# First mixture of experts: unweighed bf16 one-hots, slot weights at the silu product, expert outputs added back as three bf16 parts

## What is computed

```python
E, K, H, F = (64, 6, 256, 96)
T = 2 * 128
CAP = 2 * (T * K // E)          # 48
buf = jnp.zeros((E, CAP + 1, H), x.dtype).at[se, slot].set(x[tok])[:, :CAP]
h = jax.nn.silu(jnp.einsum('ech,ehf->ecf', buf, w_gate)) * jnp.einsum('ech,ehf->ecf', buf, w_up)
out = jnp.einsum('ecf,efh->ech', h, w_down)
gathered = out[se, jnp.minimum(pos, CAP - 1)] * valid.astype(x.dtype)[:, None]
w = topk_w.reshape(-1)[order].astype(x.dtype)[:, None]
return jax.ops.segment_sum(gathered * w, tok, num_segments=Tn)
```

## Time and profile before

| what | value |
|---|---|
| median of three runs | 692.86 us |
| profiled execution | 691.79 us |
| its span, first to last instruction | 689.9 us |
| PE busy over the span | 599.5 us (87%) |
| DVE, ACT, POOL busy | 482.6, 383.2, 330.0 us |
| mean granted TensorE clock | 0.921 |
| stage of the first experts, loop of 16 groups | 188.0 to 289.9 us |

### The profile page before, as it was taken

The page is one execution under the profiler, slowest core; times in us unless marked ns, Lnnn a source line. Parts: engine busy times, 40 slices in busy tenths (PEclk is TensorE's granted clock), DMA queues, the critical chain, the costliest instruction groups (busy, mean ns, idle before and its releaser), DMA issues. The chain is left out here.

```text
span 689.9 us, 12529 instructions
## 1 busy us (share of the span) xinstructions
PE 599.5 (87%) x4685; PEld 407.8 (59%) x4685; DVE 482.6 (70%) x793; ACT 383.2 (56%) x722; POOL 330.0 (48%) x264
## 2 busy tenths in 40 slices
PE   4976899997899999988876698888988877989997
PEld 3542445444677777676752455565555565668886
DVE  4357999995565664367686899999999956433322
ACT  4227975551432222155876799999999954321110
POOL 1009999995122332033432898989899840000000
PEclk9999999997999999999995678898878889999999
DMA  8526500000936555025563888988798738900000
GB/s 345 238 74 263 228 0 1 0 1 4 298 114 209 196 175 182 11 67 152 158 183 91 166 166 155 168 137 189 135 174 156 144 63 340 385 1 1 0 1 16
DMA packets 97090, 92.89 MB, mean 135 GB/s; under 512 B 70595, under 2 KB 88323, under 8 KB 93638
## 3 DMA queue, kind: packets, MB, share of 16 engines
q1 hardware_dynamic: 84352, 85.74, 45.7%
q10 hardware_dynamic: 12678, 6.36, 3.2%
HBM read 68.59 MB, written 6.62 MB: 109 GB/s over the span
## 5 line engine op out<-in xcount | busy, mean ns | idle before, releaser
L2074 DVE TENSOR_REDUCE d_nmax<-d_psum 128x1 f32<-128x1024 f32 x128 | 152.2, 1215 | 5.8 <-PE d_psum L2230 5.8
L2230 PE MATMUL d_psum<-kst,qT 96*128 96x512 bf16 x256 | 96.6, 477 | 31.8 <-ACT d_e L2171 12.9
L528 POOL TENSOR_TENSOR b_h<-b_h,b_cb 128x1024 f32<-128x1024 f32 x32 | 88.0, 2749 | 6.5 <-DVE b_h L578 6.0
L2054 POOL TENSOR_SCALAR d_rounded<-d_e,d_lift 128x1024 f16<-128x1024 f32 x64 | 73.2, 1144 | 13.4 <-issue 7.4
L2171 ACT ACTIVATE d_e<-d_psum,d_nmax 128x1024 f32<-128x1024 f32 x64 | 71.3, 1117 | 12.7 <-DVE d_nmax L2074 12.1
L2054 POOL TENSOR_SCALAR d_rounded<-spare,d_lift 128x1024 f16<-128x1024 f32 x62 | 70.1, 1131 | 14.4 <-ACT d_lift L2175 10.2
L578 DVE TENSOR_TENSOR_SCAN b_h<-b_dA,b_psum 128x1024 f32<-128x1024 f32 x32 | 73.2, 2286 | 2.5 <-ACT b_dA L633 2.0
L2171 ACT ACTIVATE spare<-d_psum,d_nmax 128x1024 f32<-128x1024 f32 x64 | 71.3, 1118 | 1.9 <-DVE d_nmax L2074 1.9
L633 ACT ACTIVATE b_dA<-b_dtT,b_A 128x248 f32<-128x248 f32 x128 | 53.7, 490 | 33.1 <-DVE b_h L578 28.1
L2257 PEld LDWEIGHTS d_psum<-d_ident_f,d_rounded 128*128 128x128 f16 x512 | 45.4, 123 | 32.1 <-issue 21.6
L689 PE MATMUL b_psum<-b_bdiag,b_dtx 128*128 128x512 f32 x128 | 60.2, 594 | 0.8 <-DVE b_h L578 0.8
(11 more groups left out here) (430 smaller groups left out, 1168.7 us busy)
## 6 DMA issues: line engine op xcount, KB each, us to landing
c_w<-in_w0gu SPq DMA_DIRECT2D x16, 768.0 KB, 4.8
kst<-kT_scratch SPq DMA_DIRECT2D x84, 128.0 KB, 2.7
w<-in_w SPq DMA_DIRECT2D x5, 1920.0 KB, 21.3
b_cb<-c_scratch SPq DMA_DIRECT2D x4, 2048.0 KB, 7.0
c_w<-in_w0dn SPq DMA_DIRECT2D x16, 384.0 KB, 5.5
kT_scratch<-k_kT ACTq DMA_DIRECT2D x15, 384.0 KB, 2.8
a_ctx<-in_ctx SPq DMA_DIRECT2D x2, 2048.0 KB, 19.8
k_ctxT<-in_ctxT SPq DMA_DIRECT2D x12, 256.0 KB, 3.1
```

Source lines behind the costliest of these rows:

```text
L528: nc.gpsimd.tensor_tensor(hv, hv, cv, ALU.mult).then_inc(hc_ready, 1)
L2054: nc.gpsimd.tensor_scalar(tile_of(r, j), e[j], lift[t][:, f:f + 1], HALF_ULP_ONE, ALU.mult, ALU.add).then_inc(r_ready, 1)
L2074: nc.vector.tensor_reduce(nm[:, t, m:m + 1, f:f + 1], quarter(m, j).unsqueeze(1), AX.X, ALU.max, negate=True).then_inc(nm_ready, 1)
L2230: last = nc.tensor.matmul(quarter(m, j)[:, b * 512:(b + 1) * 512], qT[0:QROWS, m:m + 1, t * P:(t + 1) * P], kst[m % 2][0:QROWS, at:at + 51 ...
```

## The change

The one-hot `pick` is now padded to 64 slots per expert itself, and goes back as it is, in bf16 and unweighed, so that POOL's weighing (`pickw`) is gone. `turn_back` is moved ahead of `gate_up` and takes group `it` in place of `it-2`; it transposes in bf16. The weights are split into three bf16 parts (five new DVE instructions before the loop), and four small matmuls per group, of 6 columns each, bring each slot's weight parts to the slot's partition. DVE sums the parts (two small reductions, `wslot`) and multiplies by them in the product with the silu, which becomes two instructions. The expert outputs are split into three bf16 parts: ACT copies the first, DVE subtracts, ACT copies the second, POOL subtracts the third. `add_back` is 12 bf16 matmuls in place of 4 fp32 ones. `back` has five buffers for three.

```diff
-        pick = [sb(f"c_pick{s}", [P, TC, GRP, CAP0], BF16) for s in range(3)]
-        pickw = [sb(f"c_pick_weighed{s}", [P, TC, GRP, HALF]) for s in range(2)]
+        pick = [sb(f"c_pick{s}", [P, TC, GRP, HALF], BF16) for s in range(3)]
...
+def split_weights(nc, dve, w, parts, rests, part_ready, rest_ready):
+
+    for q in range(K_PARTS):
+        src = ([w] + rests)[q]
+        if q:
+            dve.wait_ge(rest_ready, q)
+        nc.vector.tensor_copy(parts[q], src).then_inc(part_ready, 1)
+        if q < K_PARTS - 1:
+            dve.wait_ge(part_ready, q + 1)
+            nc.vector.tensor_tensor(rests[q], src, parts[q], ALU.subtract).then_inc(rest_ready, 1)
...
+                def split_out2(grp):
+                    s = grp % 2
+                    pool.wait_ge(out1_ready, grp + 1)
+                    nc.gpsimd.tensor_tensor(out[s][:, 2], out_rest[s][:, :, :], out[s][:, 1], ALU.subtract).then_inc(out2_ready, 1)
...
                 def choose(grp):
                     if grp >= 3:
-                        dve.wait_ge(gather_done, grp - 2)
-                        dve.wait_ge(pickw_ready, grp - 2)
+                        dve.wait_ge(back_done, grp - 2)
...
-                    nc.vector.tensor_tensor(a[grp % 2][:, :, :], silu[grp % 2][:, :, :], gu_psum[:, :, F0:],
-                                            ALU.mult).then_inc(a_ready, 1)
+                    dve.wait_ge(wslot_ready, 2 * grp + 2)
+                    for q in range(PAIRS):
+                        nc.vector.scalar_tensor_tensor(a[grp % 2][:, q, :], silu[grp % 2][:, q, :], wslot[grp % 4][:, q:q + 1],
+                                                       gu_psum[:, q, F0:], ALU.mult, ALU.mult).then_inc(a_ready, 1)
...
-                    nc.vector.tensor_copy(back[grp % 3][:, :, :], st_psum).then_inc(back_ready, 1)
-
-                def keep_out(grp):
-                    dve.wait_ge(down_done, grp + 1)
+                    nc.vector.tensor_copy(back[grp % BACKS][:, :, :], st_psum).then_inc(back_ready, 1)
+                    for h in range(2):
+                        rows_ = slice(h * HALF, (h + 1) * HALF)
+                        nc.vector.tensor_reduce(wslot[grp % 4][rows_, :], ws_psum[rows_, :, h, :], AX.X,
+                                                ALU.add).then_inc(wslot_ready, 1)
+
+                def split_out(grp):
+                    s = grp % 2
+                    dve.wait_ge(out0_ready, grp + 1)
                     if grp >= 2:
-                        dve.wait_ge(added, grp - 1)
-                    nc.vector.tensor_copy(out[grp % 2][:, :, :], out_psum).then_inc(out_ready, 1)
+                        dve.wait_ge(out2_ready, grp - 1)
+                    nc.vector.tensor_tensor(out_rest[s][:, :, :], out_psum, out[s][:, 0], ALU.subtract).then_inc(out_rest_ready, 1)
...
+                def split_out0(grp):
+                    act.wait_ge(down_done, grp + 1)
+                    if grp >= 2:
+                        act.wait_ge(added, grp - 1)
+                    nc.scalar.activation(out[grp % 2][:, 0], out_psum, ACT.Copy).then_inc(out0_ready, 1)
+
+                def split_out1(grp):
+                    act.wait_ge(out_rest_ready, grp + 1)
+                    nc.scalar.activation(out[grp % 2][:, 1], out_rest[grp % 2][:, :, :], ACT.Copy).then_inc(out1_ready, 1)
...
                     for q in range(PAIRS):
                         for t in range(TC):
-                            last = nc.tensor.matmul(acc[t], back[grp % 3][:, q, t * P:(t + 1) * P], out[grp % 2][:, q, :],
-                                                    start=False, stop=(grp == NGRP - 1 and q == PAIRS - 1),
-                                                    skip_group_check=True)
+                            for n in range(K_PARTS):
+                                last = nc.tensor.matmul(acc[t], back[grp % BACKS][:, q, t * P:(t + 1) * P], out[grp % 2][:, n, q, :],
+                                                        start=False, skip_group_check=True,
+                                                        stop=(grp == NGRP - 1 and q == PAIRS - 1 and n == K_PARTS - 1))
```

More of the change, by code:

```diff
@@ L829, in moe0_stage @@
         aT = [sb(f"c_aT{s}", [F0, PAIRS, P]) for s in range(2)]
-        back = [sb(f"c_back{s}", [P, PAIRS, T]) for s in range(3)]
-        out = [sb(f"c_out{s}", [P, PAIRS, D]) for s in range(2)]
+        back = [sb(f"c_back{s}", [P, PAIRS, T], BF16) for s in range(BACKS)]
+        out = [sb(f"c_out_parts{s}", [P, K_PARTS, PAIRS, D], BF16) for s in range(2)]
+        out_rest = [sb(f"c_out_rest{s}", [P, PAIRS, D]) for s in range(2)]
+        wparts = sb("c_w_parts", [P, TC, E0, K_PARTS], BF16)
+        wrest = [sb(f"c_w_rest{q}", [P, TC, E0]) for q in range(K_PARTS - 1)]
+        wslot = [sb(f"c_w_slot{s}", [P, PAIRS]) for s in range(4)]
         shared_silu = sb("c_shared_silu", [P, TC, F0])
@@ L931, in _ @@
                 nc.gpsimd.tensor_copy(slot[:, :], slot_i[:, :]).then_inc(slots_ready, 1)
+                for s in range(3):
+                    nc.gpsimd.memset(pick[s][:, :, :, CAP0:], 0.0).then_inc(pads_ready, 1)
                 for s in range(2):
-                    nc.gpsimd.memset(pickw[s][:, :, :, CAP0:], 0.0).then_inc(pads_ready, 1)
                     nc.gpsimd.memset(xT[s][:, :, SLOTS:], 0.0).then_inc(pads_ready, 1)
@@ L1033, in _ @@
                 weigh0(nc, step, r, w_ready)
+                dve.wait_ge(w_ready, 1)
+                split_weights(nc, dve, r.w[:, :, :], [wparts[:, :, :, q] for q in range(K_PARTS)],
+                              [rest_[:, :, :] for rest_ in wrest], wpart_ready, wrest_ready)
                 for it in range(NGRP + 4):
@@ L1036, in _ @@
                         choose(it + 2)
+                    if it < NGRP:
+                        keep_back(it)
                     if 1 <= it <= NGRP:
                         multiply(it - 1)
-                    if 2 <= it <= NGRP + 1:
-                        keep_back(it - 2)
                     if 3 <= it <= NGRP + 2:
-                        keep_out(it - 3)
+                        split_out(it - 3)
                     m, at = divmod(it - QUANTIZE_AT, 2)
@@ L1182, in gather @@
                             for q in range(3):
-                                last = nc.tensor.matmul(xt_psum[:, k, :], xp[q][:, t, k * P:(k + 1) * P],
-                                                        pick[grp % 3][:, t, :, :].rearrange("p e s -> p (e s)"),
+                                last = nc.tensor.matmul(xt_psum[:, k, :].rearrange("p (e s) -> p e s", s=CAP0),
+                                                        xp[q][:, t, k * P:(k + 1) * P], pick[grp % 3][:, t, :, 0:CAP0],
                                                         start=(t == 0 and q == 0), stop=(t == TC - 1 and q == 2))
@@ L1213, in turn_back, with pair @@
                 def turn_back(grp):
-                    pe.wait_ge(pickw_ready, grp + 1)
-                    if grp >= 1:
-                        pe.wait_ge(back_ready, grp)
+                    if grp == 0:
+                        pe.wait_ge(wpart_ready, K_PARTS)
+                    else:
+                        pe.wait_ge(wslot_ready, 2 * grp)
+                    def pair(q, t):
+                        return pick[grp % 3][:, t, 2 * q:2 * q + 2, :].rearrange("p e s -> p (e s)")
                     for q in range(PAIRS):
                         for t in range(TC):
-                            last = nc.tensor.transpose(st_psum[:, q, t * P:(t + 1) * P],
-                                                       pickw[grp % 2][:, t, 2 * q:2 * q + 2, :].rearrange("p e s -> p (e s)"),
-                                                       ident[:, :])
+                            nc.tensor.transpose(st_psum[:, q, t * P:(t + 1) * P], pair(q, t), g["identb"][:, :])
+                    for q in range(PAIRS):
+                        own = slice(grp * GRP + 2 * q, grp * GRP + 2 * q + 2)
+                        for t in range(TC):
+                            last = nc.tensor.matmul(ws_psum[:, q].rearrange("p h n -> p (h n)"), pair(q, t),
+                                                    wparts[:, t, own, :].rearrange("p h n -> p (h n)"), start=(t == 0),
+                                                    stop=(t == TC - 1), skip_group_check=True)
                     last.then_inc(back_done, 1)
@@ L1251, in _ @@
                         project_second(9)
+                    if it < NGRP:
+                        turn_back(it)
                     if 1 <= it <= NGRP:
@@ L1257, in _ @@
                         turn(it - 2)
-                        turn_back(it - 2)
                     if 3 <= it <= NGRP + 2:
```

49 lines of the change are left out of this document (28 added, 21 removed).

## The result

| | before | after |
|---|---|---|
| median, runs made together | 693.79 us (4 runs, 692.32 to 695.34) | 684.4 us (4 runs, 682.1 to 686.62) |
| ratio, 95% interval | | 0.9868 [0.9827, 0.9909] |
| profiled execution, its span | 691.79, 689.9 us | 682.87, 681.1 us |
| from the first `gather` to DVE's addition to `x` | 188.0 to 289.9: 101.9 us | 184.7 to 279.8: 95.1 us |
| mean granted TensorE clock | 0.921 | 0.92 |

The forecast was 687.0 us, and the time is inside its range. A run more than 1.5% above the fastest of its kernel counts as slow and is left out of the ratios, which happens once, for three of the ten runs with the third part on DVE, the profiled one among them.

The account below looks back on a forecast made before the run. PE was taken to set the loop's pace. Savings of 6.2 us (`add_back`) and 1.0 (`turn_back`), less 0.6 (start) and 0.7 (end), gave 5.9: from 692.86 to 687.0 us, range 683.5 to 692.0.

Parts of the forecast that it names:

- `add_back`, 12 x 0.52: Bringing outputs back in iterations 4 to 15: 12 bf16 matmuls take 1.31 us instead of 1.83, 6.2 us saved.
- `turn_back`, 16 x 0.06: One-hot transposes in all 16 groups: bf16 saves more than the four new small matmuls cost, 1.0 us saved.
- The start, 0.6 lost: Loop start: PE stalls 0.5 us for the weights' third part, then 0 to 0.5 more; bounds 0.3 and 1.3.
- The end, 0.7 lost: Last iterations: 2.8 us of stalls on the output chain, less 2.1 saved by four `add_back`; bounds 0.3 and 1.5.
- A: PE in the loop: saved more, with cheaper small matmuls, `add_back` and ends; 7.6 us saved, 685.3 us; chance 0.13.
- B: Mid-loop: output chain takes over, using up 0.78 us to spare; 690.0 us if late by 0.3; chance 0.18.
- C: Next stage's start: clock falls to 1.2 GHz for 3.5 us of work, losing 1.7 us; 688.7 us; chance 0.14.
- D: Loop iterations: DVE becomes the bound through collisions with POOL, needing up to 7.0 us; 697 us; chance 0.12 with E.
- E: `add_back` on PE: three parts no cheaper than fp32, result 695 us; no share of its own, 0.12 with D.

## Why the prediction was right

The mechanism is right and some terms are off in size. The time is right, partly by luck, as the last paragraph here shows. The loop gave 6.8 us where 5.9 were forecast. Read by starts, it divides in three: from the first `gather` to that of group 3 it went from 9.90 to 10.79 us, from there to the `gather` of group 15 from 72.21 to 65.04, and from there to DVE's addition from 19.81 to 19.32.

- *`add_back`, 12 x 0.52.* Right: 1.83 to 1.32 us, 0.51. The price of 0.109 us for a matmul of 256 columns, worked out from matmuls of 128 and 192, was 0.108 in the run with two parts. The weights' reload does not show.
- *`turn_back`, 16 x 0.06.* Too small, it is 0.14, and it was one price that was wrong. The old step was worth the 0.44 that I had given it: from `turn` to `down` there were 0.79 us and now are 0.35. The new step was put at 0.38 and costs 0.30: from `gather` to `gate_up` 1.09 us became 1.39. The four transposes take 0.22, as forecast, so the small matmuls take 0.02 to 0.03 each, and not 0.04. Where a full-width `gather` follows them, at the loop's start, four take 188.53 - 188.43 = 0.10 us; in the middle 0.18, and the other 0.08 is the gap that used to stand behind `gather`. The gaps cancel, as argued. The term was worth 2.2 us, not 1.0: the largest miss.
- *The start, 0.6 lost.* The weight parts took 1.56 us, as worked out. The trace says that PE waited 0.23 us for them, but that wait is counted from the modelled end of the matmul ahead: from its start to the next there are 188.20 - 187.70 = 0.50 us, where the same step took 191.19 - 191.08 = 0.11 before, so 0.39 were lost of the 0.5 forecast. For the second `turn_back` PE did not wait. Up to the `gather` of group 3 the stretch grew by 0.89; three new steps for one old are 3 x 0.30 - 0.44 = 0.46 of it, so 0.43 was lost, which is that one stall, and within the bounds.
- *The end, 0.7 lost.* The stalls came as forecast, 0.76, 0.16 and 1.77 us against 0.7, 0.4 and 1.7. But the stretch from the `gather` of group 15 became only 0.49 us shorter. One `add_back` (0.51) and three old `turn_back` less a new one (3 x 0.44 - 0.30 = 1.02) save 1.53, so the end itself lost 1.04: the stalls of 2.69 less 4 x 0.51, and 0.39 more. The waits leave out 0.30 of this, since they too are counted from modelled ends. From start to start the stalls are 272.39 - 270.55 - 1.01 = 0.83, 275.04 - 273.79 - 1.01 = 0.24 and 278.28 - 275.04 - 1.32 = 1.92 us, 2.99 in all against 2.8 forecast. The last 0.1 lies between the start of the last `add_back` and DVE's addition: 1.51 us where its pace is 1.32, and before, for the last two, 3.75 where it is 3.66.

With these sizes, 12 x 0.51 + 16 x 0.14 - 0.43 - 1.04 = 6.9 us, against 6.8.

The rivals. **A** (7.6 saved) was right that the small matmuls are cheaper than 0.04 and wrong on the two ends; the loop's 6.8 lie in the middle between it and the forecast. **B**, the output chain: 0.78 us to spare were forecast, after 0.12 for POOL's signal to reach PE; 0.77 less 0.14 are in the timeline, and the longer chain of the experiment shows 0.66. The chain ran 0.07 us longer than laid out and the iteration was 0.06 shorter. **C**, the clock: it did not fall behind the loop in any of the four profiles of the changed kernel; it did in the run with two parts, where 3.4 us of the next stage ran at the lower level, close to the 3.5 that the prediction guessed. **D**, DVE as the bound: its collisions are there and much larger than I thought. In an iteration with both, the key product went from 0.97 to 1.66 us and one `choose` from 0.35 to 1.20, 1.54 us more, where the prediction held that collisions add about 0.3. The Trainium skill ("SBUF — State Buffer", Who interferes with whom) says that such instructions shut each other out for a whole instruction, and the trace agrees nearly: POOL's L987 began 0.04 us ahead and ended at 233.98, and the key product, 0.68 us where it runs alone, ended 0.54 after that. So DVE needed 5.40 us in these iterations and not 4.7, and had 0.13 to spare. All of PE's buffers were ready in time, so nothing came of it, but that is luck more than foresight: what helped were the lighter iterations in between, at 3.82. The experiment with the third part on DVE shows how near it was: it had to stand in DVE's queue behind the keys, and PE then waited. **E** fell with `add_back` at 1.32 us.

The whole program. All 27 runs of the changed kernel have a mean of 686.8 us, and 61 of the kernel before 691.9: 5.1 us less, a ratio of 0.993, where the loop alone would give 0.990. Outside the loop the four profiles of the changed kernel took 585.9, 591.2, 591.7 and 590.7 us, the two of the kernel before 588.0 and 589.1. Part of the first measured 9.4 us is therefore chance. In the first profile of before, the clock fell to 0.50 ahead of the stage, and in the first one after it did not:

```profile
164.00:168.00 4.00, 2.23 (x9) 1.68 (x10) 1.12 (x2) 0.00 (x0) 0.47 (x1) 1.00 0.00 0
```

The first `gather` came at 188.0 us in the one and 184.7 in the other, and between 184.8 and 188.0 in the other profiles, whose kernels are nearly alike up to there. Taken by itself, the spread of the rest, 6 us, is too large for so few profiles to say whether part of the loop's 6.8 us is given back. The timed runs say more: from their scatter, the 5.1 us are known to about 1.1 (95%), so some 1.7 us seem to be given back. The first four runs alone gained 9.4, the later ones 3 to 5, so the batches differ by more than their scatter and the bound is too narrow. But the experiments lean the same way. The loop was 14.0 us shorter with two parts and the whole 9.5 (6.1 to 12.9); with POOL's work doubled the loop was 2.3 longer and the whole 5.0 (2.8 to 7.3); with `add_back` in fp32, 1.5 shorter and the whole 2.9 (1.2 to 4.6), where nothing seems to be given back. The cause is open. The granted clock goes with it: its mean over the runs that list it is 0.918 for the kernel before (57 runs), 0.914 for the changed one, 0.909 with two parts and 0.921 with the fp32 `add_back`, and of the kernel before the runs at 0.911 or less took 693.9 us on average and those at 0.923 or more 689.9. No run separates the change from the clock in the later stages.

So the forecast of 687.0 us and the 686.8 of all runs agree better than their parts: the loop gave 0.9 us more than forecast, the rest seems to have taken back about 1.7, which the prediction's sum had at nothing (its rival C put such a loss at the start of the next stage, where the clock did not fall), and the kernel before lies at 691.9 and not at 692.86. The 684.4 of the first four runs stands where rival A put it, mostly by chance: of A's reasons only the cheaper small matmuls came true. That the change gains 6.8 us in the loop is shown; that the gain in the whole lies near 5 us is the best value that the runs give.

## What to carry to other kernels

When a split or a conversion is moved off the bounding engine, lay out its chain in time on every engine in its order, find the margin to where the bounding engine needs it, and then do the same for the first and the last iterations, where nothing hides it; there the old form may be the better one. Count the load of an in-order queue per iteration and not on average. Compare a stage with the same stage across repeats before the whole program's difference is explained by the change, and do not take the stage's gain for the whole's: the runs of the whole have to show it.

## What the runs showed that I had not expected

- A matmul of 128 rows with 256 bf16 columns, with its own stationary operand each time, costs 0.108 us; an fp32 one costs 0.46 us. Three bf16 parts are 0.7 of the fp32 time.
- A key product of 512 elements on DVE takes 0.68 us alone, 0.97 when POOL's subtraction began 0.74 us ahead of it, and 1.66 when that began 0.04 ahead. No wait of PE comes of it in the changed kernel.
- The same program with the same instructions took 585.9 to 591.7 us outside the changed stage, while the loop itself was the same within 0.2 us in four profiles. Loop times were some thirty times sharper than the rest.
- A wait that the trace gives for PE is counted from a modelled end. Where PE restarts after a wait, it was short by 0.07 us behind `down` and by 0.15 behind `add_back`; the full stall is read from start to start.
